# A gated coupling network on one core: first layer kept as a product and its twist, output turned row by row

## The reference, cut to what matters

```
def _twist(x):
    o_r, o_i, p_r, p_i = jnp.split(x, 4, axis=-1)
    return jnp.concatenate([p_r, -p_i, -o_r, o_i], axis=-1)
...
gf = _global_net(x.mean(axis=1, keepdims=True), ...)      # one number per batch
out = x
for _ in range(3):
    tf = _coupling_net(out, ...)    # 256 -> 256 -> 128 -> 64 -> 1: three gelu layers, then a sigmoid
    combined = 0.7 * gf + 0.3 * tf
    coupling = 0.1 + adaptive_range * (combined - 0.5) * 2.0
    out = out + coupling * _twist(out)
return out
```

## Time and profile before

| | us |
|---|---|
| median of 3 runs (707.22 to 707.89) | 707.75 |
| the profiled execution, its own time | 706.14 |
| its span (first to last instruction) | 704.3 |
| PE busy in the span | 688.3 (98%) |
| DVE busy | 384.4 (55%) |
| ACT busy | 287.6 (41%) |
| POOL busy | 132.9 (19%) |

### The profile page before, as it was taken

The page is one execution under the profiler, slowest core; times in us unless marked ns, Lnnn a source line. Parts: engine busy times, 40 slices in busy tenths (PEclk is TensorE's granted clock), DMA queues, the critical chain, the costliest instruction groups (busy, mean ns, idle before and its releaser), DMA issues.

```text
span 704.3 us, 11180 instructions
## 1 busy us (share of the span) xinstructions
PE 688.3 (98%) x3616; PEld 475.1 (67%) x3617; DVE 384.4 (55%) x951; ACT 287.6 (41%) x599; POOL 132.9 (19%) x111
## 2 busy tenths in 40 slices
PE   8999999999999999999999999999999999999996
PEld 7777777776754444688999746656556777777765
DVE  4688877788724454788777657212333333333331
ACT  3555434543544655766777541110323222222220
POOL 3100000000000000600000104661123334333333
PEclk9999999999999999999999999999999999999999
DMA  9781000000052000004800201423582666666643
GB/s 292 194 250 34 1 0 0 0 0 0 1 167 73 0 5 5 1 1 167 312 0 1 89 2 49 140 86 113 171 222 30 166 153 175 168 164 164 165 101 35
DMA packets 54934, 65.15 MB, mean 92 GB/s; under 512 B 11583, under 2 KB 37905, under 8 KB 54895
## 3 DMA queue, kind: packets, MB, share of 16 engines
q1 hardware_dynamic: 47806, 55.31, 24.6%
q0 software_dynamic: 7088, 9.35, 7.7%
HBM read 48.48 MB, written 16.00 MB: 92 GB/s over the span
## 4 chain that ended last, share of the span: by engine, by line
PE 92%; DVE 3%; ACT 1%; issue 1%; DMA 1%; POOLq 0%; SPq 0%; DVEq 0%; ACTq 0%; POOL 0%
PE ps L567 82%; PE ps L570 10%; DVE stats L1701 1%; DMA early<-in_wk 1%; DVE x_rows L1965 0%; POOLq L133 0%; ACT work L1285 0%; DVE work L1992 0%; DMA work<-expert_rows 0%; DVE x_rows L2001 0%; DVE work L1834 0%; DVE maxes L1832 0%; ACT early L1448 0%; ACT middle L1319 0%; DVE rden L1990 0%
## 5 line engine op out<-in xcount | busy, mean ns | idle before, releaser
L567 PE MATMUL ps<-middle,work 128*128 128x256 f32 (+4 forms) x656 | 177.4, 420 | 1.2 <-ACT work L1285 0.8
L1285 ACT ACTIVATE work<-ps 128x512 f32<-128x512 f32 (+3 forms) x209 | 83.1, 437 | 200.3 <-PE ps L570 183.6
L567 PEld LDWEIGHTS ps<-middle,work 128*128 128x128 f32 (+1 forms) x656 | 115.7, 183 | 48.3 <-issue 29.2
L567 PE MATMUL ps<-late,work 32*128 32x154 f32 (+5 forms) x880 | 141.9, 345 | 0.6 <-ACT work L1285 0.6
L533 POOL DMA_INDIRECT out_rows<-masks x47 | 70.4, 1498 | 152.3 <-DMA out_rows<-masks 56.7
L567 PEld LDWEIGHTS ps<-late,work 128*128 128x128 f32 (+2 forms) x880 | 92.1, 178 | 6.4 <-issue 3.4
L567 PE MATMUL ps<-work,late 128*128 128x256 f32 (+1 forms) x416 | 83.0, 352 | 0.6 <-ACT work L1285 0.5
L570 PE MATMUL ps<-consts_sb,work 128*128 128x128 f32 (+1 forms) x564 | 80.1, 275 | 1.8 <-DVE work L1992 1.2
L499 POOL TENSOR_TENSOR rstd<-var_eps,minus_half 128x8 f32<-128x8 f32 (+1 forms) x10 | 13.9, 1392 | 358.1 <-DVE var_eps L1716 358.1
L570 PEld LDWEIGHTS ps<-consts_sb,work 128*128 128x128 f32 (+1 forms) x564 | 65.1, 140 | 22.0 <-issue 11.6
L567 PE MATMUL ps<-early,late 128*128 128x512 f32 (+2 forms) x192 | 77.6, 608 | 0.3 <-ACT early L1435 0.3
(11 more groups left out here) (226 smaller groups left out, 720.4 us busy)
## 6 DMA issues: line engine op xcount, KB each, us to landing
late<-in_w SPq DMA_DIRECT2D x40, 512.0 KB
early<-in_w SPq DMA_DIRECT2D x16, 512.0 KB, 9.7
expert_rows<-work SPq DMA_DIRECT2D x36, 130.0 KB, 2.9
work<-expert_rows SPq DMA_DIRECT2D x36, 130.0 KB
middle<-in_w SPq DMA_DIRECT2D x8, 512.0 KB, 7.9
out_rows<-x_rows SPq DMA_DIRECT2D x4, 512.0 KB, 3.2
x_rows<-in_x SPq DMA_DIRECT2D x2, 768.0 KB, 10.6
late<-in_ws SPq DMA_DIRECT2D x3, 512.0 KB, 4.0
```

Of the source, the lines that this page charges most:

```text
L567: return nc.tensor.matmul(o, l, r, start=start, stop=stop, **kw)
L1285: return nc.scalar.activation(o, i, ACT.Copy)
```

## The change

**First layer.** The product of a group's state with the first weights is made once (`net1("y", n)`, kept by ACT's copies in `ys`), and so is the product of its twist (`net1("z", n)`, with the twisted and signed weights `wz` that DVE makes, kept in `zs`). That is 8 `net1` in place of 12. In cycles 2 and 3 no `net1` runs: DVE (`turn_y`) adds c times zs to ys, into the place of `st_x`, and POOL (`turn_z`) takes c times ys off zs, once per group (cycle 3 needs no new zs). `act1` of cycles 2 and 3 reads `st_x` instead of a PSUM bank.

**The couplings.** The scale and shift after the tanh move from ACT to DVE (the line `f_c` of `turn_y`). The last layer is still made over all partitions for cycles 1 and 2 (`net4`, 4 in place of 6 pairs), and besides for every cycle by token (`couplings_by_row`, 6 calls): hidden columns of 128 tokens are the weights, one column of the last layer is the moving operand, so that the result has a token per partition. ACT takes the tanh of these (`by_row`).

**The output.** `st_x` no longer holds the state, so the transposes `to_rows` and the additions `ffn_out` are gone. The three cycles of a token come down to two numbers (`two_cycles`, `three_cycles` on DVE, on 128x8 elements), and the output row is a combination of the normed row `xng` and its quarters, swapped: `out_row` on DVE for 4 tiles (three instructions a tile), `out_rows_` on POOL for the other 12 (five instructions a tile: three products into a scratch row, two additions into `xs`). DVE takes these tiles' statistics in `row_stats`.

**Moved with it.** `NORMS` counts by tile of a batch; two of its groups are halved. `su1(1)` stands before `to_columns(2)`, `su1(0)` near the end of the net. SP's load of `w2s` waits for the last `turn_y`, and that of `w13` for the last row of POOL. `h3` and `tt` have a buffer for each use. The second cross-attention's steps 2 to 5 are plain `step1` on PE.

```diff
-NORMS = [(0, 1), (1, 2), (2, 4), (0, 2), (2, 4), (0, 1), (1, 2), (2, 4), (0, 2), (2, 4)]
+NORMS = [(0, 2), (2, 4), (4, 8), (0, 4), (4, 8), (0, 1), (1, 2), (2, 4), (4, 8), (0, 4), (4, 8)]
...
+        def turned_row(eng, pi, k, j, sync):
+            g = pi + 2 * k
+            o, i = xs[:, 4 * g + j, :], xng[:, g, j, :]
...
+            sync(eng.scalar_tensor_tensor(o, i, a, o, ALU.mult, ALU.add))
+            eng.scalar_tensor_tensor(o4[:, 0::3, :], i4[:, 2:0:-1, :], b, o4[:, 0::3, :], ALU.mult, ALU.add)
+            return eng.scalar_tensor_tensor(o4[:, 1:3, :], i4[:, 3::-3, :], c, o4[:, 1:3, :], ALU.mult, ALU.add)
...
+            def turn_z(n):
+                g, c = ffn_group(n), tt[n]
+                pool.wait_ge(q["f_y"], 2 * n + 2)
+                after(pool, q["f_z1"], n)
+                pseq.mark(nc.gpsimd.tensor_tensor(pool_u[0], c, ys[:, g, 0, :], ALU.mult))
+                pseq(nc.gpsimd.tensor_tensor(pool_u[1], c, ys[:, g, 1, :], ALU.mult))
+                nc.gpsimd.tensor_tensor(zs[:, g, 0, :], zs[:, g, 0, :], pool_u[0], ALU.subtract)
+                nc.gpsimd.tensor_tensor(zs[:, g, 1, :], zs[:, g, 1, :], pool_u[1], ALU.subtract).then_inc(q["f_z1"], 1)
...
+            for n in range(NG):
+                turn_z(n)
+            out_rows_(0, 0, [(0, 2)])
+            reciprocal_roots(5)
+            out_rows_(0, 1, [(1, 2)])
+            reciprocal_roots(6)
+            out_rows_(0, 2, [(0, 3), (1, 3)])
+            reciprocal_roots(7)
+            out_rows_(1, 4, [(k, j) for j in range(4) for k in range(2)])
...
+            def couplings_by_row(p):
+                pe.wait_ge(q["f_a3"], p + 1)
...
+                for j in range(4):
+                    for k in range(2):
+                        rows = slice(64 * k, 64 * k + 64)
+                        at = 4 * (p // 2) + j
+                        last = mm(ps[:, 4 * k + p % 2, at:at + 1], h3[p][rows, P * j:P * j + P], fw4[rows, 0:1])
...
-            for p in range(2, 6):
-                net1(2 * p, 0)
-                net3(p - 1)
-                net1(2 * p, 1)
-                net4(p - 1)
-                net1(2 * p + 1, 0)
-                net1(2 * p + 1, 1)
-                net2(2 * p)
-                net2(2 * p + 1)
...
+            net1("y", 2)
+            net1("y", 3)
+            net2(2)
...
+            net2(3)
+            net1("z", 2)
+            net3(1)
+            net2(4)
+            net4(1)
+            net2(5)
+            net1("z", 3)
+            net3(2)
+            net4(2)
+            couplings_by_row(0)
+            couplings_by_row(1)
+            net2(6)
+            net2(7)
+            couplings_by_row(2)
+            net3(3)
+            net2(8)
+            net4(3)
+            net2(9)
+            couplings_by_row(3)
+            net3(4)
+            couplings_by_row(4)
+            su1(0)
+            net2(10)
+            net2(11)
             net3(5)
...
+            def turn_y(n):
...
+                v.tensor_scalar(c, c, cpl[:, 0:1], base, ALU.mult, ALU.add).then_inc(q["f_c"], 1)
...
+                for o in range(2):
+                    seq.mark(v.tensor_tensor(dve_u[o], c, zs[:, g, o, :], ALU.mult))
+                for o in range(2):
...
+                    v.tensor_tensor(st_x[:, o, g, :], (ys[:, g, o, :] if n < NG else st_x[:, o, g, :]), dve_u[o],
+                                    ALU.add).then_inc(q["f_y"], 1)
...
+            row_stats(0, 4)
+            variances(7)
+            dve.wait_ge(q["rstd_done"], 8)
```

413 lines of the change are left out of this document (243 added, 170 removed).

## The result

The changed kernel takes 712.09 us (median of 15 runs, 709.00 to 715.48), the kernel before 707.22 in runs beside them (15, 705.37 to 711.46). The ratio is 1.0063, 95% interval 1.0045 to 1.0082: slower by 4.9 us, where 4.6 us less was forecast, and outside the range (699.3 to 706.8). The profiled execution took 712.9 us, its span 711.0 (before 704.3).

The account below looks back on a forecast made before the run. PE, busy 98% of the span, was taken to bound the kernel. Net -4.6, attention start +2.6, steps 2 to 5 -3.2 and +0.6 sum to -4.6 us: 707.75 to 703.2 us, range 699.3 to 706.8.

Parts of the forecast that it names:

- the four steps: Second cross-attention, steps 2 to 5: period from 7.22 to 6.41 us, -3.2 us, and +0.6 for statistics of POOL's rows.
- the clock: Rival, chance 0.03: clock falls to 1.2 GHz as PE waits at 247 to 279 us; about 711 us.
- PE's work in the net: PE up to columns1(0, 0): -17.9 us gone, +9.0 for six calls by token, +4.3 of waits, net -4.6 us.
- the prediction's lower bound: Call by token in the net: loads of the two row halves go side by side, 0.9 us a call.
- I put nothing for it here: POOL holding DVE at the net's end: 0.2 to 1.6 us later, put at nothing, 1 us in the range.
- The contention: Rival, chance 0.12: DVE and POOL hold each other up at the net's end, 2 to 3 us later, 705.5 us.
- the 17: DVE's tail at the net's end, from the tanh of group-cycle 6 (262.5) to xn0(0, 0): about 17 us.
- DVE has almost no slack: Net's end: DVE's xn0(0, 0) is done at about 279.5 us, as late as PE at 279.8.
- The start: Start of the second cross-attention: new DVE work and a wait for POOL's root make att1(0, 0) late, +2.6 us.
- the handovers: Rival, chance 0.13: ACT-PE-ACT-DVE handovers in cycles 2 and 3 each 0.1 to 0.2 us dearer, +3.5 us, 706.7 us.
- the two rivals of late engines: DVE and POOL in each other's way (705.5 us, chance 0.12) and dearer handovers in cycles 2 and 3 (706.7 us, 0.13).

Follow-up runs that it names:

- e1: Changed kernel with three more keep_warm before columns1(0, 0) and two more behind pv1(0, 0), both in PE's waits: 707.79 us, ratio to before 1.0013.
- e10: Kernel before with 32 added products of one moving column (64 records) ahead of net2(8): 717.56 us, ratio 1.0151.
- e7: Changed kernel with the four turn_z on DVE instead of POOL and added products of 384 columns on PE in the net: 709.65 us, ratio 1.0033.
- e14: Changed kernel with couplings_by_row(0) moved behind net2(6) and couplings_by_row(1) behind net2(7), nothing added: 712.80 us, ratio 1.0077.
- e4: Changed kernel with three_cycles(1) moved in front of soft(0, 0), and POOL's rows' statistics and variance in front of soft(0, 1), on DVE: 708.23 us, ratio 1.0009.
- e13: Changed kernel with POOL's first two output rows behind the roots 5 and 6 instead of ahead of them: 708.12 us, ratio 1.0015.
- e5: Changed kernel with xn0(0, 0) and xn0(0, 1) on DVE moved in front of out_row(0, 1), out_row(1, 1), their statistics and variances(6): 706.53 us, ratio 0.9990.
- e9: Kernel before without its keep_warm(2, 1), four products of 512 columns ahead of columns1(0, 0): 710.94 us, ratio 1.0043.
- e6: Changed kernel with only DVE's order changed, the moves of e5 and e4 together: 705.73 us, ratio 0.9964.

## Why the prediction was wrong, step by step

By the stretches, forecast and measurement are 11.3 us apart: 5.0 up to `columns1(0, 0)`, 4.7 from there to the end of `pv1(0, 0)`, 1.3 in the four steps, and 0.3 in the others. Two steps of the prediction failed, both terms that the sum held at nothing: the clock, and DVE beside POOL.

- **PE's work in the net: right, even too careful.** A call by token is 1.06 us alone, and two in a row are 1.85 with the clock up (e1) and 2.15 here, where it fell under the last of them. The forecast took 1.5, from the 0.081 us of a row of 36 records with the changes of the array on top. That row was misread. It is not `pv1` alone, but 20 records of `pv1` and 16 of `scores1`, which have 32 rows (groups of the kernel before, 296 to 299.2 us):

```profile
L567 PE MATMUL ps<-late,work 128*128 128x51 f32 x10 | 1.7, 280 | 0.0
L567 PE MATMUL ps<-late,work 128*128 128x34 f32 x10 | 1.7, 265 | 0.0
L567 PE MATMUL ps<-late,work 32*128 32x154 f32 x16 | 0.8, 315 | 0.0
```

  The 20 of `pv1` take 2.25 us (296.20 to 298.45), 0.112 each, as in e10, and the 0.081 is a mean over two kinds. So the row did not speak against the figure of the Trainium skill that the prediction quotes and sets aside for it. A call is eight pairs of halves, each pair at 0.112: 0.9 us from start to start, the prediction's lower bound, and 1.06 to the end of the last record. Six calls are 6.4 us, not 9.0. The waits up to the last call are 0.66 + 0.79 + 2.01 + 0.79 + 0.78 = 5.0 us, against 6.3; and before, PE was idle 0.85 us in that stretch, where the forecast's prices left 2.0. The two errors cancel by luck: waits cost 4.2 us more, for the 4.3 of the sum. With a full clock the list would have ended near 277 us, as it did in e7, before the forecast 279.8.
- **The clock: the larger step that failed.** It stood as a rival with 0.03, since PE "never waited there" before. That was evidence about a kernel without waits, used for one with six. Behind the 3.19 us wait the low level cost 4.7 us (e1 gave back 5.3 at the first `att1`), behind the 2.21 us wait about 1.5 (first period 7.99, then 6.45, 6.58, 6.60). In the net it lengthened `net2(6)` and `(7)` by 3.0 us (6.73 against 3.70 in e7), `su1(0)` by 0.8 and `net2(10)` and `(11)` by 0.9. These 4.7 us are not a loss by themselves: in e14, e1 and e4 the first of them was elsewhere, and the net ended within 0.3 us of where it did. So the rival's price, some 10 us of work at twice the time and 711 us, came near by luck. It placed all of it between 247 and 279 us, and what reached the time lay in the main behind 284.
- **"I put nothing for it here": failed.** The contention of DVE and POOL was to fit into DVE's slack, with 1 us in the range. Beside POOL a `turn_y` took 7.2 us (251.53 to 258.75, its scale and shift with it) for the forecast 3.0. The end of `xn0(0, 0)` is 5.2 us later than the forecast 279.5, in two halves. The coupling of group-cycle 6 came at 265.11 for 262.5; this half has two covers, PE's low clock and DVE beside POOL, and with both gone it came at 262.35 (e7). And DVE's tail from there took 19.6 us (to 284.7) where 17 was forecast; without POOL in e13 it took 16.7. So the 17 held as a total, for a DVE that works alone, though the terms that the prediction lists for it come to 14 only. The only row of before showed one instruction held once; I read it as the price of one collision, when it was the rate for as long as both work.
- **"DVE has almost no slack": right, and not followed up.** A tail that ends with PE makes PE wait as soon as anything is late. Nor did I ask what in it `xn0(0, 0)` needs: half of the rows it doesn't, and e5 shows 5.6 us in that order.
- **The start: right.** Forecast 2.6 us, measured 2.4 at `att1`, with the fall of the clock on top. **The four steps: right in e4**, 26.25 us against 28.92 before, -2.7 for the forecast -2.6; in the changed kernel 27.62, as the first is slow.
- **The rivals were treated as alternatives.** The contention (0.12), the handovers (0.13) and the clock (0.03) are one chain: what makes PE wait brings the clock down behind it. The forecast and the two rivals of late engines had the end of the net between 280 and 283.5 us. An end as late as measured, 5.0 us, would alone have given some 708 by the forecast's sum; the way from there to 712 is in the main the clock behind the waits.

## What to carry to other kernels

Where a change takes work from the engine that bounds and leaves it waiting, price each new wait twice: its own length, and the products behind it at the lower clock, where they come in short bursts; here waits of 2.0 to 3.2 us at the attention's start cost 1.5 to 5 us more than themselves. It is a price for a risk: the wait of 2.01 us at 261 us, with twelve records of 128x512 right behind it, cost nothing more (clock 1.00 from 260 to 270). Before giving work with two SBUF inputs to POOL, add to DVE's path what DVE loses beside it: here 10.9 us for 10 us of help. And of a tail that sets a stage's end ask of each instruction whether the waiting one needs it: other orders, and `turn_z` on DVE, made 712 into 700 us with no work added.

## What the runs showed of the hardware

- Taking 2 us of idle products out of the kernel before made it 3.6 us slower (e9); adding five products to the changed one made it 4.3 us faster (e1).
- The granted clock fell in a stretch of products with one moving column in which PE shows no wait (e10), and one net, the same on PE, had its fall at 250 us in some kernels (e5, e6, e13) and at 259 in others (e1, e4).
- Records with weights of 128 rows and one moving column start 0.112 us apart at the upper level of the clock and 0.213 at the lower (e10).
- DVE and POOL, both with two SBUF inputs of 128x512, took 1.65 us a turn where alone they take 0.65 and 1.27.
- Two products of one column with weights of 64 rows, in the two halves of the array, go side by side: 32 records took 1.85 us with the clock up (e1), where 32 of 128 rows take 3.6 (e10).
